# A three-layer decoder on one core: scores of every pair one slot early, transposes ahead of the previous pair's product with the values

## The reference

```python
x = x + attn(layernorm(x), in_proj_weight, out_proj_weight)      # 16 heads of 8, causal
x = x + xattn(layernorm(x), ctx, Wq, bq, Wk, bk, Wv, bv, W1, b1, W2, b2)
        # 16 heads over 64 context tokens, no mask, then relu(out @ W1 + b1) @ W2 + b2
x = x + ffn(layernorm(x), ...)
        # h = x + rope_attention(rmsnorm(x)), causal; h + moe(rmsnorm(h)): 2 of 8 experts, hidden 384
```

## Time and profile before

| what | us |
|---|---|
| median of 3 runs | 831.12 (828.60 to 832.57) |
| the profiled execution | 831.9 |
| its span, first to last instruction | 829.9 |
| PE busy in it | 701.2 |
| DVE busy | 505.4 |
| ACT busy | 370.4 |
| POOL busy | 277.0 |
| mean granted clock of TensorE | 0.928 |

### The profile page before, as it was taken

One profiled execution on the slowest core, in us unless ns is written; L12 is line 12 of the kernel. 1 busy time (PEld: TensorE's weight loads), 2 busy tenths in 40 slices (PEclk: granted clock), 3 DMA queues, 4 the chain that ended last, 5 costly groups with the idle time before them and its releaser, 6 DMA issues.

```text
span 829.9 us, 19929 instructions
## 1 busy us (share of the span) xinstructions
PE 701.2 (84%) x7442; PEld 477.4 (58%) x7443; DVE 505.4 (61%) x1126; ACT 370.4 (45%) x831; POOL 277.0 (33%) x396
## 2 busy tenths in 40 slices
PE   3999999999899899999997889950479999999950
PEld 2566666665666556566564556640346766667740
DVE  4577776766676565757666485738825445444437
ACT  4455555545354445453525433442324444444424
POOL 6001020102101212313212241122667777777633
PEclk9999999999999899999999899965579999999995
DMA  4308000000000010010101001010121111111118
GB/s 109 109 22 246 16 15 25 15 24 15 14 24 15 18 45 2 27 38 23 40 15 35 5 15 40 27 51 1 60 88 48 50 49 47 47 51 48 43 60 267
DMA packets 36734, 39.15 MB, mean 47 GB/s; under 512 B 11792, under 2 KB 26960, under 8 KB 36528
## 3 DMA queue, kind: packets, MB, share of 16 engines
q1 hardware_dynamic: 32112, 28.74, 11.3%
q0 software_dynamic: 4544, 9.32, 3.8%
HBM read 20.80 MB, written 10.94 MB: 38 GB/s over the span
## 4 chain that ended last, share of the span: by engine, by line
PE 60%; DVE 17%; issue 7%; POOL 7%; ACT 5%; DMA 2%; SPq 0%; DVEq 0%; POOLq 0%; ACTq 0%
PE ps_s L663 11%; PE ring L1058 7%; PE ring L1042 7%; PE ps_s L1030 6%; PE ring L679 6%; PE ring L1008 5%; DVE rmax L1213 5%; DVE shifted L1217 5%; PE ring L671 4%; PE ring L932 3%; POOL room L595 2%; PE ring L995 2%; PE ps_s L1020 2%; PE ring L941 2%; ACT fres L1108 1%
## 5 line engine op out<-in xcount | busy, mean ns | idle before, releaser
L1213 DVE TENSOR_REDUCE rmax<-ps_s 128x16 f32<-128x1024 f32 x96 | 116.8, 1217 | 77.2 <-PE ps_s L1030 77.2
L1093 ACT ACTIVATE probsT<-ring 128x512 f32<-128x512 f32 x192 | 104.1, 591 | 132.7 <-PE ring L1042 132.6
L1058 PEld LDWEIGHTS ring<-vbd,probsT 128*64 128x64 f32 x3072 | 99.6, 140 | 53.6 <-issue 35.7
L1217 DVE TENSOR_TENSOR shifted<-ps_s,rmax 128x1024 f32<-128x1024 f32 x96 | 117.6, 1225 | 9.9
L1058 PE MATMUL ring<-vbd,probsT 128*64 128x18 f32 x3072 | 108.6, 214 | 4.6 <-DVE att L1228 2.0
L1042 PE MATMUL ring<-const,shifted 128*128 128x128 f32 x768 | 108.6, 286 | 0.0
L663 PE MATMUL ps_s<-w_exp,room 128*128 x284 | 106.6, 499 | 0.6 <-ACT room L713 0.6
L1030 PE MATMUL ps_s<-room,qT 64*64 64x512 f32 x768 | 100.6, 604 | 0.0
L746 DVE SCALAR_TENSOR_TENSOR room<-room,ps_s 128x384 f32<-128x384 f32 x71 | 39.3, 554 | 99.9 <-ACT room L719 99.9
L1042 PEld LDWEIGHTS ring<-const,shifted 128*128 128x128 f32 x768 | 85.4, 144 | 3.4 <-issue 0.5
L616 POOL DMA_INDIRECT y_dram<-room,scatter_rows x71 | 69.9, 984 | 44.0 <-DVE room L755 42.8
(11 more groups left out here) (176 smaller groups left out, 958.2 us busy)
## 6 DMA issues: line engine op xcount, KB each, us to landing
room<-kS SPq DMA_DIRECT2D x192, 32.0 KB, 1.9
room<-y_dram SPq DMA_DIRECT2D x16, 256.0 KB, 6.2
room<-in_x SPq DMA_DIRECT2D x8, 256.0 KB, 3.7
hn_dram<-hn SPq DMA_DIRECT2D x8, 256.0 KB, 2.3
base_dram<-base SPq DMA_DIRECT2D x8, 256.0 KB, 2.4
room<-base_dram SPq DMA_DIRECT2D x1, 2048.0 KB, 8.0
out<-room SPq DMA_DIRECT2D x8, 256.0 KB, 3.6
cin<-in_ctx SPq DMA_DIRECT2D x8, 192.0 KB, 3.1
```

The lines of the kernel that those rows point to most:

```text
L1058: last = mm(ring[u.bank][rows, c:c + 2 * (D + 1)], probsT[p % 2][:, k, rows], vbd[r][:, at:at + 2 * (D + 1)], start=True, stop=True)
L1093: nc.scalar.activation(probsT[p % 2][:, 4 * g:4 * g + 4, :], ring[u.bank][:].rearrange("p (k c) -> p k c", c=P), ACT.Exp, scale=SCALE)\
L1213: V.reduce_max(rmax[p % 2][:], ps_s[p % 2][:], AX.X).then_inc(rmax_ready, 1)
L1217: V.tensor_tensor(shifted[p % 2][:], ps_s[p % 2][:], rmax[p % 2][:].unsqueeze(2).broadcast_to([P, HEADS, SEQ]), ALU.subtract)\
```

## The change

`walk` is rewritten, and with it the order of instructions on PE and DVE, the numbers of the ring's uses and so the banks. (1) The scores of the next pair stand at the head of every slot, also in slot 3, where they are those of the next job's pair 0; `shift` of them stands ahead of `normalise` on DVE. (2) In every slot `exps(n, p)` stands ahead of `attend` of the previous pair. (3) All eight additions of the last stage are on DVE, and POOL has none.

```diff
@@ walk @@
-            if p < SUB - 1:
-                scores(n, p + 1)
+            following = (n, p + 1) if p < SUB - 1 else (n + 1, 0)
+            if following[0] < N_JOBS:
+                scores(*following)
             steps(steps_at(n, p, 0))
-            if p < SUB - 1:
-                shift(n, p + 1)
+            if following[0] < N_JOBS:
+                shift(*following)
+            exps(n, p)
             if p > 0:
                 attend(n, p - 1)
             elif n > 0:
                 attend(n - 1, SUB - 1)
-            exps(n, p)
-            if p == SUB - 1 and n + 1 < N_JOBS:
-                scores(n + 1, 0)
-                shift(n + 1, 0)
             steps(steps_at(n, p, 1))
@@ combine_dve @@
-            if t in POOL_SUMS:
-                continue
             dve.wait_ge(weighed, (t + 1) * SUB)
             dve.wait_ge(first_added, (t + 1) * SUB)
```

More of the change, by code:

```diff
@@ L409, in _build @@
     PARTS = 8
-    POOL_SUMS = (0, 1, 3, 4, 6)
     base_loaded = sem("base_loaded")
@@ L416, in _build @@
     summed = sem("summed")
-    summed_pool = sem("summed_pool")
     stored = sem("stored")
@@ L582, in experts_sp @@
         for t in range(TILES):
-            if t in POOL_SUMS:
-                sp.wait_ge(summed_pool, POOL_SUMS.index(t) + 1)
-            else:
-                sp.wait_ge(summed, t + 1 - len([x for x in POOL_SUMS if x < t]))
+            sp.wait_ge(summed, t + 1)
             sp.dma_start(out_t[t], residual[:, t * SUB:(t + 1) * SUB, :]).then_inc(stored, 16)
@@ L792, in combine_dve @@
             V.tensor_tensor(residual[:, sl, :], y0[:, sl, :], y1[:, sl, :], ALU.add).then_inc(summed, 1)
[L794 to L801, removed]
     block = ctx.enter_context(nc.Block())
@@ L1422, in _ @@
         experts_pool(pool)
-        combine_pool(pool)
 INPUTS = ["x", "ctx_768", "L0_attn_in_proj_weight", "L0_attn_out_proj_weight",
```

## The result

| | before | after |
|---|---|---|
| median, us | 831.85 (828.60 to 832.90, 4 runs) | 852.25 (850.35 to 853.50, 4 runs) |
| the profiled execution, us | 831.9 | 850.35 |
| its span, us | 829.9 | 848.3 |
| mean granted clock | 0.928 | 0.915 |

The ratio is 1.024, with an interval of 1.021 to 1.028: 20.4 us slower by the medians. The forecast was 12.2 us, 843.3 (834 to 854), so the result lies in the last 2 us of its range.

The account below looks back on a forecast made before the run. PE was taken as the bound while the 24 jobs run, its waits being for banks with late readers. Idle +11.2, clock +2.5 and last stage -1.5 gave +12.2 us on 831.9, 844.1, as a median 843.3 us, range 834 to 854.

Parts of the forecast that it names:

- (a): Jobs 9, 14, 16, 18: `h1` also waits for the first exponential, so `xT` starts one `h1` later; +4.1 us.
- (b): Jobs 10, 15, 17: `v` waits for slot 1's first exponential, partly offset by an earlier chain and slot 3; +1.5 us.
- (c): Jobs 19, 21: `v` itself waits for the late exponentials, with `v` and scores still to run before `xT`; +3.6 us.
- (d): Job 20: the `qr` wait goes, but `v` waits for the exponential and `h1` starts later; +1.2 us.
- (e): Single places in jobs 2, 4, 6, 8, 11, 12, 13, 22 and 23, gains and losses together; +0.6 +0.5 +0.5 +0.8 -1.6 us.
- half clock: PE at 1.2 GHz behind idle stretches: one and a half more such stretches net, +2.5 us, between 0 and +12.
- last stage: Additions moved from POOL to DVE, four of them on DVE's path, save 4 x 0.35; -1.5 us, between -0.5 and -2.
- the prediction's own test: Wrong if slot 1's exponentials end before PE finishes `wo`, or the half-clock share differs by over 15 us.
- now meet DVE late: Jobs 22 and 23: the last transposes wait for DVE, giving back +0.3 us of the gain there, -1.6 us in all.
- Faster: Rival: waits for DVE go and exponentials are in time, 814 us, or 822 if half remains; chance 0.08.
- No change: Rival: longer waits eat the clock and last-stage gains, or late starts are absorbed, 829 to 835 us; chance 0.17.
- Clock: Rival: every new idle stretch brings 3.4 to 6.8 us at half clock, 853 us and above; chance 0.12.

Follow-up runs that it names:

- after_norm_late: The changed kernel with ACT applying the next norm behind the slot's exponentials instead of ahead of them: 814.12 us, 0.981 of the kernel before.
- late_four: The changed kernel with the norm applied behind the exponentials only in jobs 9, 14, 16 and 18: 871.88 us on a slower chip, 1.011 of the kernel before.
- idle_filled: The changed kernel with 27 unused products on PE in 12 of its idle stretches: 834.22 us, 1.001 of the kernel before.
- walk_only: The kernel before with the changed walk alone, five additions of the last stage staying on POOL: 852.33 us, 1.023 of the kernel before.

## Why the prediction was right, and where its size was off

**Direction and mechanism.** As forecast, `h1` and `v` wait for a bank whose reader is ACT, behind `ap`, behind POOL. after_norm_late, which touches only ACT's order, shows it: 38 us.

**The terms of the sum, one by one** (idle before each step, from the two timelines):

| term | forecast | measured |
|---|---|---|
| (a) `h1` in jobs 9, 14, 16, 18 | +4.1 | +2.5 |
| (b) `v` in jobs 10, 15, 17 | +1.5 | +1.3 |
| (c) `v` in jobs 19, 21 | +3.6 | +3.7 |
| (d) job 20 | +1.2 | +1.3 |
| (e) single places | +0.8 | -0.1 |
| idle, sum | +11.2 | +8.7 |
| half clock | +2.5 | +8.1 |
| last stage | -1.5 | -0.9 |

In (a) three places came as worked out, 1.9 to 2.98, 1.9 to 2.99 and 1.46 to 2.47: each one `h1` more. The fourth, job 18, for which the rows were shown, did not, and the forecast that `h1` would stand behind its idle stretch held only with 0.83 us. Timeline of PE in job 18, slots 1 and 2:

```profile
416.53 1.91 PE L1012 MATMUL ps_s<-room,qT 64*64 64x512 f32 x8
...
424.78 1.10 PE L973 MATMUL ring<-oT,w 128*128 128x512 f32 x2 [0.83 <-ACT probsT L1075]
```

A stretch of half clock at 416.5 made PE's own work late (scores 1.91 us there, 1.03 without it), so PE came later to a bank that was free at the same time. What is missing in idle time, some 1.6 us, is paid for as half clock. In (e) 0.5 us of the first `attend` went that I had not looked at, and jobs 22 and 23 came out at -1.7 for the forecast's -1.6 by luck: two waits of 0.84 us for the exponentials and one of 0.41 us went beside the `qr` wait, not one, and 1.4 us came back, not 0.3.

(c) and (d): the three long stretches, 6.04, 5.33 and 5.87 us. The text named two over 5 us, jobs 19 and 21; by its own working (d) had a third, 4.05 us of three waits joined into one of 5.3; it counts it only under the clock, as "three over 4".

```profile
450.76 1.98 PE L923 MATMUL ring<-w_f,xT 128*64 128x64 f32 x32 [6.04 <-ACT probsT L1075]
452.67 1.76 PE L1012 MATMUL ps_s<-room,qT 64*64 64x512 f32 x8
...
478.96 1.98 PE L923 MATMUL ring<-w_f,xT 128*64 128x64 f32 x32 [5.33 <-ACT probsT L1075]
...
510.32 1.98 PE L923 MATMUL ring<-w_f,xT 128*64 128x64 f32 x32 [5.87 <-ACT probsT L1075]
```

**The step that failed is the clock**, "one and a half more half-clock stretches net": +2.5 us, where it was +8.1, inside the range given for it (0 to +12). Idle time came 2.5 us under its term and half clock 5.6 us over, so the sum is nearer than its parts, which is luck. By the prediction's own test (a half-clock share that differs by over 15 us) the step was wrong: 28.0 us of the walk ran at half clock before, 50.6 after. The 8.1 have two halves.

Up to job 22 there were six stretches of half clock before and nine after, three more where the forecast had one and a half, though of the twelve idle stretches of 1.9 us or more that it expected only ten came. Up to there, half clock cost 12.1 us before and 16.1 after. Before, three of the six idle stretches of 1.9 us or more had it behind them; after, eight of ten had. It came as 3.4 us at 211.7, 235.6, 348.3, 375.6, 399.5 and 416.5 (the last behind no idle stretch), and as 6.8 us over each of the three long ones. Two of the nine, in the columns of rows 14:

```profile
211.70:215.10 3.40, 3.40 (x13) 2.40 (x12) 0.00 (x0) 2.06 (x5) 0.00 (x0) 0.51 0.00 0
...
447.30:454.10 6.80, 3.33 (x40) 2.13 (x40) 0.36 (x4) 5.06 (x12) 2.86 (x5) 0.50 0.01 2
```

PE was busy for all 3.4 us of the first and for half of the second, which began while PE stood idle. So the first cost 1.5 us and the second 1.6 (the other long ones 2.8 and 2.4; and in the kernel before 6.8 us of half clock behind 2.35 and 2.60 us cost about 3 us each). In these rows the cost does not grow with the idle stretch. The price of 1.6 us for 3.4 us was right, the count was not.

The other +4.1 us stood in no term. In job 23 the prediction gave +0.3 us to transposes that "now meet DVE late". They waited 1.42 us, and at 556.5, right behind, half clock set in for the last 9.6 us of the walk; before, it set in at 546.9, in the walk's last 0.7 us.

```profile
553.67 1.11 PE L1040 MATMUL ring<-vbd,probsT 128*64 128x18 f32 x32
556.20 1.74 PE L1024 MATMUL ring<-const,shifted 128*128 128x128 f32 x8 [1.42 <-DVE shifted L1199]
557.86 1.90 PE L1040 MATMUL ring<-vbd,probsT 128*64 128x18 f32 x32
```

Of the kernels with this wait all but one had half clock within 2 us of it (late_four had none until its walk's end); of the six that keep `attend` ahead of `exps`, and so do not have it, none had more than 0.7 us there. No run takes that wait away alone, so the cause of the last 9.6 us is argued and not shown.

By the rule of the Trainium skill ("TensorE: Matmul & The Clock Gate", section "Why this matters for your kernels") only the three longest stretches would have met half clock. In after it stood behind 2.24, 2.31, 2.47 and 2.98 us too. The rule's advice to keep PE fed is borne out by idle_filled, its length of gap is not.

**What is left.** The span's +18.4 us are the +12.2 of the forecast, with +5.6 for the clock, -2.5 for idle time, +0.6 for the last stage, -0.7 for work, and three terms that it did not have: start +2.4, experts' stage +1.3, routing -0.4. The last stage gave 0.9 of 1.5 (the prediction's own 4 x 0.35 is 1.4): the 2.21 us of rows 15 became 1.13, as worked out, but in two tiles DVE now waits for ACT's weighing.

```profile
833.45 0.69 DVE L783 TENSOR_TENSOR room<-room 128x512 f32<-128x512 f32 x1 [0.17 <-ACT room L768]
834.06 1.13 DVE L778 SCALAR_TENSOR_TENSOR room<-room,weight 128x128 f32<-128x128 f32 x4
835.66 0.69 DVE L783 TENSOR_TENSOR room<-room 128x512 f32<-128x512 f32 x1 [0.46 <-ACT room L768]
```

**The rivals.** *Faster* did not come, but its mechanism, exponentials in time, is what after_norm_late makes, and it gave the 814 us that the rival had named. That the number is the same is chance: the rival took 14.1 us of waits away, and the run has 17.3 us less idle time than before and about 3 us less half clock. *No change* fell with its argument: the work at full clock is the same within 0.7 us, so PE had nothing in hand for absorbing late starts, though its weight loads were busy for less than two thirds. *Clock* was nearest by its numbers: it had some 25 us more at half clock, +10 us and 853 us, against 22.6 us, +5.6 us over the forecast's term, and 852.25. But not every new idle stretch brought half clock, and half of the excess came in job 23, where the rival had nothing. Its chance of 0.12 looks low beside the rows of before, which had half clock three times behind idle stretches of 1.46 us and less.

**Open.** What decides whether half clock follows an idle stretch: behind the 2.95 us ahead of job 12's `xT` after had none, and walk_only, with the same walk, had 6.8 us of it (its half clock cost 23.0 us in all, against 20.2). One trace for each kernel cannot tell how far this shifts between executions of the same kernel. Nor was it tried why the experts' stage takes 31 to 34 us longer on one chip.

## What to carry to other kernels

When a change reorders uses of a ring of banks, list for each use the reader of the use before it in its bank, and what stands ahead of that reader on its own engine: here four or eight activations that waited for POOL. Then move that late work rather than PE's; the same new order of PE cost 2.4% without this and gained 1.9% with it. Price an idle stretch of PE with the clock it takes along, short ones as well, and test that price with unused products in the idle time before rearranging anything.

## What the hardware showed beyond this

Unused products of PE in idle stretches held the granted clock at 1.00 up to 540 us, where it had fallen to 0.50 nine times: 27 of them, each about 0.9 us, took 18 us off the changed kernel, and 12 took 1.2% off the kernel before. Half clock behind an idle stretch of 2.24 us and over one of 6.04 us cost about the same, 1.5 and 1.6 us.
